# A four-stage decoder kernel: P x V directly behind the scores, and another order of copies in both attention stages

## The reference: what is computed

```python
# stage "a": 16 heads of 32 features, biases, mask of ones
v = (values @ Wv + bv).reshape(N, L, H, D)
k = (keys @ Wk + bk).reshape(N, L, H, D)
q = (query @ Wq + bq).reshape(N, L, H, D)
energy = jnp.einsum('nqhd,nkhd->nhqk', q, k)
energy = jnp.where(mask == 0, jnp.float32(-1e+20), energy)
attn = jax.nn.softmax(energy / np.sqrt(D), axis=3)
out = jnp.einsum('nhqk,nkhd->nqhd', attn, v).reshape(N, L, E)
return out @ Wo + bo
...
x = x + _L0_xattn_ref(ctx_1024, ctx_1024, _layernorm(x, axis=-1), ...)   # stage a, 16 heads
x = x + _L0_ffn_ref(_layernorm(x, axis=-1), ...)                         # stage b
x = x + _L1_xattn_ref(_layernorm(x, axis=-1), ctx_1024, ...)             # stage c, 8 heads of 64
x = x + _L1_ffn_ref(_layernorm(x, axis=-1), ...)                         # stage m
```

## Time and profile before

| | us |
|---|---|
| median of 3 runs | 2343.01 (2342.31 to 2343.47) |
| the profiled execution, its own time | 2342.86 |
| its span from the first to the last instruction | 2341.1 |
| PE busy in the span | 2085.5 (89%) |
| DVE busy | 1454.9 (62%) |
| ACT busy | 1072.0 (46%) |

### The profile page before, as it was taken

How to read it: one execution, slowest core, us unless ns; L and a number is a source line. 1 busy time by engine, 2 the same in 40 slices (tenths; PEclk the granted TensorE clock), 3 DMA queues, 4 the chain that set the end, 5 groups by cost and what they waited for, 6 DMA issues and landing times. The chain is left out here.

```text
span 2341.1 us, 47494 instructions
## 1 busy us (share of the span) xinstructions
PE 2085.5 (89%) x14941; PEld 1588.2 (68%) x14976; DVE 1454.9 (62%) x4087; ACT 1072.0 (46%) x2781; POOL 676.2 (29%) x1179
## 2 busy tenths in 40 slices
PE   5999999999996389898995899999999979999986
PEld 5777777777774344444444788888888768888844
DVE  5878778787785477777772656565555533333354
ACT  4666666666664643333342544445444422222224
POOL 2323233233222545555542221221212111111100
PEclk8999999999998699999997999999999989999999
DMA  4111211111100611212114021211211092222200
GB/s 164 51 40 39 75 39 38 64 50 38 52 23 30 227 50 58 63 55 66 54 54 145 29 74 37 73 45 64 69 40 54 28 318 86 81 80 73 67 5 0
DMA packets 91344, 158.11 MB, mean 68 GB/s; under 512 B 11248, under 2 KB 21488, under 8 KB 90752
## 3 DMA queue, kind: packets, MB, share of 16 engines
q1 hardware_dynamic: 91264, 157.10, 19.8%
HBM read 123.50 MB, written 33.57 MB: 67 GB/s over the span
## 5 line engine op out<-in xcount | busy, mean ns | idle before, releaser
L479 ACT ACTIVATE a_probs<-a_probs,a_negm 128x256 f32<-128x256 f32 x512 | 254.0, 503 | 187.0 <-DVE a_negm L580 187.0
L399 POOL TENSOR_SCALAR a_probs<-a_probs,a_rinv 128x256 f32<-128x256 f32 x256 | 133.8, 534 | 449.9 <-DVE a_rinv L596 449.9
L819 PE MATMUL a_pt<-a_ident,a_probs 128*128 128x128 f32 x1024 | 160.9, 281 | 56.0 <-ACT a_pT L487 37.7
L580 DVE CUSTOM_DVE_ANT_0 a_probs<-a_s,a_mbias 128x256 f32<-128x256 f32 x512 | 188.6, 418 | 2.1 <-PE a_s L802 2.1
L399 POOL TENSOR_SCALAR c_probs<-c_probs,c_rinv 128x256 f32<-128x256 f32 x128 | 67.1, 534 | 393.1 <-DVE c_rinv L596 393.1
L819 PEld LDWEIGHTS a_pt<-a_ident,a_probs 128*128 128x128 f32 x1024 | 123.7, 144 | 82.6 <-issue 61.3
L1126 ACT ACTIVATE b_raw<-b_g,b_xs 128x512 f32<-128x512 f32 x128 | 88.1, 688 | 182.0 <-PE b_g L1297 182.0
L479 ACT ACTIVATE c_probs<-c_probs,c_negm 128x256 f32<-128x256 f32 x256 | 127.4, 502 | 90.3 <-DVE c_negm L580 90.3
L1297 PE MATMUL b_u<-b_wu,b_raw 128*128 128x512 bf16 x495 | 130.7, 380 | 40.5 <-DVE b_raw L1209 39.6
L1209 DVE SCALAR_TENSOR_TENSOR b_raw<-b_u,b_xs,b_raw 128x512 f32<-128x512 f32 x128 | 93.2, 748 | 62.5 <-ACT b_raw L1126 55.0
L1297 PE MATMUL b_g<-b_wg,b_raw 128*128 128x512 bf16 x497 | 128.2, 379 | 2.3 <-ACT b_raw L1117 1.6
(11 more groups left out here) (297 smaller groups left out, 4942.9 us busy)
## 6 DMA issues: line engine op xcount, KB each, us to landing
m_ew<-in_L_ffn_w_dram SPq DMA_DIRECT2D x24, 512.0 KB, 8.8
a_cbuf<-in_ctx_dram SPq DMA_DIRECT2D x16, 512.0 KB, 5.4
a_xbuf<-in_x_dram SPq DMA_DIRECT2D x16, 512.0 KB, 4.3
a_resb<-in_x_dram SPq DMA_DIRECT2D x16, 512.0 KB, 3.6
x<-a_resb SPq DMA_DIRECT2D x16, 512.0 KB, 2.8
b_xbuf<-x SPq DMA_DIRECT2D x32, 256.0 KB, 2.7
b_raw<-x SPq DMA_DIRECT2D x32, 256.0 KB, 2.7
x<-b_raw SPq DMA_DIRECT2D x32, 256.0 KB, 2.0
```

The source lines that it names most:

```text
L399: last = nc.gpsimd.tensor_scalar(pr, pr, rinv[:, s, QT + t:QT + t + 1], 0.0, ALU.mult, ALU.add)
L479: nc.scalar.activation(pr, pr, ACT.Exp, bias=negm[:, s, h % 2, t:t + 1], scale=-1.0, accum_out=ssum[:, s, QT * (h % 2) + t:QT * (h % 2) + ...
L580: nc.vector.tensor_tensor_reduce(out=probs[:, s, h % 2, t], in0=s_bank[h][:, t * SEQ:(t + 1) * SEQ], in1=mbias[:, el.par], scale=-sm_scale ...
L819: last = nc.tensor.transpose(pt_bank[:, kt * SEQ + t * P:kt * SEQ + (t + 1) * P], probs[:, s, m, t, kt * P:(kt + 1) * P], ident[:])
```

## The change

PV_AFTER and SLOTS of stage a are changed, and so is the order of calls in the loop bodies of ACT and DVE. These bodies serve stage c too, where the two tables stay as they were.

- PE, stage a alone: PV moves from behind T1 to behind T0 and the scores. In quad 0 the slot behind T1, which was empty, gets o0a, the slot behind T2 has o0b and tc1, and the slot behind T3 has o1a.
- ACT, both stages: the copy of T1 and attn_hi stand ahead of the high parts of the slot behind T0 (before: the high parts, then the copy of T1, then attn_hi).
- DVE, both stages: scores_out of head 0 stands ahead of the low parts left from the quad before. mask_bias moves from the start of quad 0 to quad QUADS // 2 - 1 (quad 1 in stage a, quad 0 in stage c), where it stands behind the copy of T2 and ahead of the low parts of the slot behind T1. In stage a attn_lo stands ahead of the low parts of the slot behind T0 and of scores_out of heads 2 and 3.

```diff
         if QUADS == 4:
-            SLOTS = [[["tc0"], [], ["o0a", "o0b"], ["tc1", "o1a"]],
+            SLOTS = [[["tc0"], ["o0a"], ["o0b", "tc1"], ["o1a"]],
                      [["o1b"], ["tx0", "v0a"], ["v0b", "tx1"], ["k0a"]],
...
-        PV_AFTER = {1: -1} if QUADS == 4 else {1: -1, 2: 0}
+        PV_AFTER = {0: -1} if QUADS == 4 else {1: -1, 2: 0}
...
                         if more:
                             exps(ne, nq, 0)
+                        probs_out(el, q, 1)
+                        attn_hi_after(el, q, 0)
+                        attn_hi_after(el, q, 1)
                         hi_of_slot(el, q, 0)
-                        probs_out(el, q, 1)
-                        attn_hi_after(el, q, 1)
                         if more:
                             exps(ne, nq, 1)
...
                         probs_out(el, q, 0)
+                        if more:
+                            scores_out(ne, nq, 0)
                         if q > 0:
                             lo_of_slot(el, q - 1, 3)
                         elif has_before(el):
                             lo_of_slot(el.plus(-1), QUADS - 1, 3)
-                        if q == 0 and el.has(1):
-                            mask_bias(el.plus(1))
                         if more:
-                            scores_out(ne, nq, 0)
                             scores_out(ne, nq, 1)
+                        attn_lo_after(el, q, 0)
                         lo_of_slot(el, q, 0)
...
                         probs_out(el, q, 2)
+                        if q == QUADS // 2 - 1 and el.has(1):
+                            mask_bias(el.plus(1))
                         lo_of_slot(el, q, 1)
```

## The result

| | us |
|---|---|
| before, median of 5 runs | 2342.96 (2340.34 to 2343.47) |
| changed, median of 5 runs | 2403.83 (2402.28 to 2404.88) |
| ratio | 1.0262, 95% interval 1.0248 to 1.0276 |
| predicted | 2387, range 2366 to 2412 |

The time lies in the range and on the side that was forecast. The loss is 61 us where 44 were worked out. Four landmarks say where it came in. The start of the last output projection of stage a moved from 750.07 to 776.31 us (+26.2), the first transposes of stage c from 1249.73 to 1274.65 (+24.9), the first transposes of stage m from 1884.47 to 1946.92 (+62.4), and the end from 2341.1 to 2402.6 (+61.5). So stage a lost 26 us (13 predicted), stage c 37.5 (31 predicted), and stages b and m moved by about 1 us each, the other way.

The account below looks back on a forecast made before the run. PE, busy for 89% of the span, was taken to bound the kernel, so its waits count. From the profiled 2342.86 us, stage a adds 13 and stage c 31, giving 2387 us, range 2366 to 2412.

Parts of the forecast that it names:

- Stage c, the order on ACT: Stage c: tx0 1.8 us late, waiting for tc0's low part; k projection 2.1 us later per element; +31 us in all.
- rival 1: Clock falls in stage c too, 1.54 us each: +9 us at six elements, +22 at all 14; chance 0.16.
- Stage a, quad 0: T2's wait of 2.40 us goes (2.5 start to start), T3 newly waits 0.7: -1.8 us per element.
- Stage a, quad 1: tx1 waits 2.45 us behind DVE's chain, where 0.2 was lost before: +2.25 us per element; mask row alone half.
- Stage a, quads 2 and 3: T3 of quad 2 waits 1.6 us against 0.5 before, +1.1 us per element; quad 3 unchanged, 0.
- The reserve of T0: Stage a: next T0 has 0.1 to 0.2 us to spare behind ACT's copy of T3; costed nothing, 0.3 an element if gone.
- Stage a, PV behind the scores: PE's own time without waits: one transpose group per quad gets the shorter follower, gain 0 to 0.7 us per element, 0.7 taken.
- Stage a, the clock: Clock term left unchanged at six falls of 1.54 us, 9 us; bounds -9 with no falls, +12 with all 14.
- rival 2: Stage a's new waits don't come: it gains 64 us, more than stage c's 31 us loss; 2310 us; chance 0.06.
- (3): Stage a: tx1 waits only 1.2 us, T3 of quad 2 none: -21 us, 2353 total; chance 0.12 together with (4).
- (4): Stage c: late high parts of tc0 and tc1 don't hold tx0 up, nothing lost; 2356 us; chance 0.12 together with (3).
- (5): Whole kernel: gains of 31 us in stage a meet stage c's loss, no change within 0.2%; chance 0.04.

## Why the prediction was right, and where it was not

**Stage c, the order on ACT: right.** The step was that tx0 is held up by 1.8 us, because the high parts come behind T1 and PV. It waits 1.77, 14 times, and putting ACT's calls back takes 33 us away, the falls of the clock with them. The wait before k was forecast at 1.1 and is 0.91. The element without a fall of the clock takes 1450.88 - 1411.85 = 39.03 us, from one k projection to the next, 2.1 more than the 36.92 between two like rows of before (1562.71 - 1525.79), as forecast.

**Stage c, the clock: a part of rival 1.** The granted clock fell behind tx0's wait in six of 14 elements. In four of them the transposes of tx show it, which take 1.71 us or more instead of 1.24; in the other two PV behind them does, with 1.98 and 1.97 us instead of 1.08. One of the four in the changed kernel, and a window behind it, with the columns of the earlier trace rows and a granted clock of 0.50:

```profile
1486.29 1.71 PE L762 MATMUL c_x<-c_ident,c_xn 128*128 128x128 f32 x8 [1.77 <-DVE c_cT L627]
...
1488.00:1490.00 2.00, 2.00 (x11) 1.22 (x11) 1.57 (x7) 1.57 (x5) 0.00 (x0) 0.50 0.00 0
```

In such an element the wait before k doesn't appear, since PE comes there later by itself, and k starts at 1569.07 where it would have been at 1568.55. A fall costs 0.5 to 0.6 us here, 3.4 us in all, and not the 1.54 each that rival 1 took from stage a. The Trainium skill (TensorE: Matmul & The Clock Gate, section on why this matters for your kernels) warns only of longer idle gaps; the trace disagrees here too, with 1.77 us of idle ahead of these falls.

The 14 elements and their falls are 33 of stage c's 37.5 us. Another 2.5 are in the first element (1349.33 - 1324.73 = 24.60 us against 22.06 before), where 1.3 were forecast: tx0 waits 1.90 us there instead of 0.54, and PV behind it takes 1.80 us instead of 1.08. The last 2.1 lie ahead of the first transposes of the probabilities (50.1 us from the start of the stage against 48.0). They are not from the order of the lists, since the kernel with the lists of before in stage c takes 49.9 there; their cause stays open.

**Stage a, quad 0: the mis-sized term.** T3's wait was put at 0.7 from start to start, and it is 374.98 - 373.75 - 0.49 = 0.74. But the step "the wait of 2.40 us goes. What is late next is T3" left out o1a. o1 writes the bank of o0, and with one half of o0 earlier and o1a alone behind T3, PE reaches it before DVE has added the rows of o0, which stands behind a normalisation. From T3 (329.25) to o1a (330.72) it takes 1.47 us instead of 0.36: 1.1 us an element, 15.5 in the stage. The quad gains 0.65 us, not 1.8, and this term alone is what the element was off by: it got 2.0 us longer without a fall of the clock (45.70 against 43.70), not 0.9. Two experiments show it: o1a's wait is there with the filled slot alone, and it goes when the rows of o0 are added first. A second step about this quad was wrong, that of the mask row: "In quad 0 it stood where DVE had time". The mask row took 1.34 us there, and the run with GpSimd's addition moved shows that 1.05 of the 2.40 us of wait at T2 hung on it.

**Stage a, quad 1: the right total by a wrong step.** The prediction had a wait of 2.45 us at tx1. Measured are 1.92 at v0a (338.95 - 336.62 - 0.41) and 0.40 at tx1, together 2.3, against 0.2 before. The step that failed is again a bank: "Behind it stand, in order, the row addition of o1" named the addition that v0a needs, and at the right time, but not that v0a waits for it. The mask row, which the text called half of the price, costs 0.28 us and not 1.25. tx1 came out at 10.47 us after T0, where 10.6 was worked out, only because the two errors cancel: T2 and its copy are 0.9 us later, behind v0a, and the mask row is 1.0 shorter. That the total agrees is luck: the prediction gave "tx1 doesn't wait" as a sign that it is wrong, and of tx1's 2.4 us 0.26 are left.

**Stage a, quads 2 and 3: right.** T3 of quad 2 is 1.65 us late from start to start (354.35 - 351.20 - 1.5), against 1.6; quad 3 has no wait. The chain named (copy of T1, attn_hi, high part of k0, then DVE) is the one that was there, though attn_hi was only a part of it: with attn_hi first 1.13 us of idle stay, and they go when the low part of k0 is moved behind the copy. The reserve of T0, which the prediction named, is what gives out then: T0 of quad 3 waits 0.54 us.

**Stage a, PV behind the scores: right.** The waits above, 0.74 + 1.1 + 1.92 + 0.40 + 1.65 = 5.8 us, leave 45.7 - 5.8 = 39.9 us of an element. Before, 43.70 less 2.5, 0.2 and 0.5 is 40.5. So PE's own time fell by 0.6 us, where the bound of 0.7 was taken, and PV does start 0.92 us behind the scores (333.68 - 332.76), as a projection did. With PE's part of the change alone the element still takes 43.70 us: the waits took this back.

**Stage a, the clock: wrong, the good way.** The term was left at 9 us, with the reason that a wait of 2.45 replaces one of 2.40. With the waits in fact spread over five places of 0.3 to 1.7 us, the granted clock stayed at 1.00 between 160 and 660 us, and the 9 us were saved. An element is 45.7 us against 44.35 on average before, falls included: 19 of the 26 us of the stage. Of the other 7 the first elements have 3.4 (the first T3 of quad 2 stands at 80.19 instead of 76.82 us) and the last element the rest; the prediction took 0 for both. In the last element T1 and T2 no longer have PV between them, and T3 waits up to 2.83 us. Why each of its waits has the length it has was not taken apart.

**The rivals.** That the new waits of stage a don't come (2), that stage a gains in part (3), and that stage c loses nothing (4) are out, and so is no change in sum (5). What rival 2 needed, DVE's attn_lo not waiting for the copy of T1, is what the kernel with attn_hi first does, and with stage c as before it does beat the kernel before, by 0.5%.

**The total.** That the time came out within 17 us of the forecast owes something to errors that cancel: in stage a o1a was left out (+15.5), the ends of the stage were taken at nothing (+7), and the clock gave its 9 us back.

## What to carry to other kernels

When work is moved on the engine that bounds the kernel, list for each moved unit the buffer that it writes and who must have read it before; a unit that comes earlier makes the readers of its buffer urgent, and a filled gap comes back at the next buffer unless their order is moved as well. In a list that an engine works through in order, nothing that waits for late work belongs ahead of something that others already wait for, however little the engine has to do. A body of code shared by two stages needs the check for each.

## What the runs showed of the hardware

An instruction of DVE that turns 128x256 integers from SBUF into floats in SBUF takes 0.28 us alone and 1.34 us when it comes upon an addition of GpSimd on 128x512, 14 times in the kernel before. One of them started at 313.29 and ended at 314.63, 0.15 us after the second of GpSimd's two additions (311.96 + 2.52 = 314.48). The normalisation shows it on a smaller scale. Of DVE's two instructions the first starts ahead of GpSimd and takes 0.35 us, and the second starts beside it and takes 0.58, again until 0.15 us after GpSimd's end (319.93 + 0.56 = 320.49):

```profile
319.79 0.35 DVE L600 TENSOR_SCALAR a_probs<-a_probs,a_rinv 128x256 f32<-128x256 f32 x1
...
319.93 0.56 POOL L399 TENSOR_SCALAR a_probs<-a_probs,a_rinv 128x256 f32<-128x256 f32 x1 [5.45 <-DVE a_rinv L596]
...
320.06 0.58 DVE L600 TENSOR_SCALAR a_probs<-a_probs,a_rinv 128x256 f32<-128x256 f32 x1
```

DVE's instructions that read PSUM didn't show this: the copy of T0 took 0.69 us beside the same addition (311.90 to 312.59), and the two low parts of q1 0.87 us together inside it (312.51 to 313.38). The Trainium skill (SBUF — State Buffer, section SBUF: two separate sides) says that GpSimd and a DVE instruction in a two-port mode share a pair of ports as an exclusive lock, and that the later one is blocked until the earlier is done. In which mode these instructions run is in no trace; for the rest the trace agrees, down to the end of the instruction, and the run with the addition moved shows the cause.

A wait of 2.40 us lowered the granted clock in six of 14 elements of the kernel before, waits of 1.73 and less in stage a of the changed one in none of the elements between 160 and 660 us, and one of 1.77 in stage c in six of 14. With the one line that split the long wait in two the element got 0.13 us shorter, and the kernel 8 us faster: most of the gain came from the clock.
